# Four transposes instead of two in each small PSUM tile, and one wide copy out of it

## What is computed

```python
xn = _layernorm(x, axis=-1)
Q = xn @ W1 + b1;  K = xn @ W2 + b2;  V = xn @ W3 + b3
attn = softmax(Q @ K.T / sqrt(1024))          # 4096 x 4096 for each batch element
attn_out = (attn @ V) @ W4 + b4
# feed-forward on the same xn: two 512x512 matrices W_real, W_imag, unfolded from small factors
out_real = xn_real @ W_real.T - xn_imag @ W_imag.T + bias_real
out_imag = xn_real @ W_imag.T + xn_imag @ W_real.T + bias_imag
x = x + attn_out + concat(out_real, out_imag)
```

## Time and profile before

| | us |
|---|---|
| median of the runs | 1701.88 |
| the profiled execution, slowest core with what lies around its span | 1703.39 |
| its span, first to last instruction, slowest core (core 3) | 1701.8 |
| spans of the 8 cores | 1689.6 to 1701.8 |
| TensorE matmuls booked as busy | 1553.4 (91%) |
| VectorE | 757.2 (44%) |
| ScalarE | 483.5 (28%) |
| GpSimd | 128.7 (8%) |

### The profile page before, as it was taken

The page is one execution under the profiler, slowest core; times in us unless marked ns, Lnnn a source line. Parts: engine busy times, 40 slices in busy tenths (PEclk is TensorE's granted clock), DMA queues, the critical chain, the costliest instruction groups (busy, mean ns, idle before and its releaser), DMA issues.

```text
span 1701.8 us, 25375 instructions; the slowest of 8 cores (1689.6 to 1701.8 us)
## 1 busy us (share of the span) xinstructions
PE 1553.4 (91%) x8496; PEld 763.4 (45%) x8496; DVE 757.2 (44%) x1863; ACT 483.5 (28%) x873; POOL 128.7 (8%) x107
## 2 busy tenths in 40 slices
PE   1668899998999999999999999999999999999998
PEld 1323565655444444444444444444444444444443
DVE  3212332423455445535553555355445535553554
ACT  0101333333322222222332322322322232332322
POOL 2000111112000000000000000000000000000000
PEclk9859999999999999999999999999999999999999
DMA  9324121213311101111111110111101111110001
GB/s 177 48 62 40 73 75 51 75 50 100 87 38 44 45 26 61 39 38 38 38 38 38 38 50 26 50 38 38 50 26 54 47 38 38 38 38 26 26 26 38
DMA packets 69531, 83.48 MB, mean 49 GB/s; under 512 B 39699, under 2 KB 49947, under 8 KB 69406
## 3 DMA queue, kind: packets, MB, share of 16 engines
q1 hardware_dynamic: 56030, 42.01, 8.5%
q10 hardware_dynamic: 9216, 33.56, 6.0%
q0 software_dynamic: 4160, 6.29, 2.4%
HBM read 69.27 MB, written 18.87 MB: 52 GB/s over the span
## 4 chain that ended last, share of the span: by engine, by line
PE 89%; DVE 4%; DMA 2%; issue 2%; SPq 2%; ACT 1%; DVEq 0%; POOL 0%; ACTq 0%; POOLq 0%
PE po L659 13%; PE po L557 13%; PE po L663 13%; PE sp_a L557 7%; PE sp_b L557 6%; PE pf L588 3%; PE sp_a L422 3%; PE sp_a L524 3%; PE sp_b L422 3%; PE sp_b L524 3%; PE pf L446 3%; PE po L446 3%; PE ptA L630 2%; PE ptB L630 2%; DVE QXT L402 2%
## 5 line engine op out<-in xcount | busy, mean ns | idle before, releaser
L663 PE MATMUL po<-V,ETs 128*128 128x512 bf16 x1024 | 388.0, 379 | 0.0
L659 PE MATMUL po<-V,ETs 128*128 128x512 bf16 x1024 | 388.0, 379 | 0.0
L557 PE MATMUL po<-KT,QXT 128*128 128x512 bf16 x1024 | 231.5, 379 | 0.0
L618 DVE TENSOR_REDUCE r<-Et 128x1 f32<-128x512 bf16 x256 | 173.5, 678 | 31.6 <-ACT Et L614 31.4
L614 ACT ACTIVATE Et<-Ssb,ngm 128x512 bf16<-128x512 f32 x256 | 164.2, 709 | 57.6 <-DVE ngm L578 47.2
L378 POOL TENSOR_SCALAR xnn<-xg,rstd,nmr 128x1024 bf16<-128x1024 f32 x64 | 76.6, 1201 | 1253.6 <-DVE nmr L374 1253.6
L557 PEld LDWEIGHTS po<-KT,QXT 128*128 128x128 bf16 x1024 | 100.2, 98 | 120.8
L570 DVE TENSOR_REDUCE mx<-po 128x1 f32<-128x512 f32 x128 | 88.5, 692 | 132.7 <-ACT Ssb L567 132.7
L567 ACT ACTIVATE Ssb<-sp_a 128x512 f32<-128x512 f32 x64 | 38.2, 597 | 369.0 <-PE sp_a L557 369.0
L663 PEld LDWEIGHTS po<-V,ETs 128*128 128x128 bf16 x1024 | 100.0, 98 | 94.5
L659 PEld LDWEIGHTS po<-V,ETs 128*128 128x128 bf16 x1024 | 99.9, 98 | 94.5
(11 more groups left out here) (92 smaller groups left out, 1780.2 us busy)
## 6 DMA issues: line engine op xcount, KB each, us to landing
xg<-x ACTq DMA_DIRECT2D x64, 512.0 KB, 3.7
xr<-x SPq DMA_DIRECT2D x32, 512.0 KB, 3.5
out<-xr SPq DMA_DIRECT2D x32, 512.0 KB, 2.6
KT<-W POOLq DMA_DIRECT2D x2, 2048.0 KB, 49.6
Ssb<-W SPq DMA_DIRECT2D x8, 512.0 KB, 6.4
Wproj<-W POOLq DMA_DIRECT2D x1, 2048.0 KB, 25.7
scr<-V SPq DMA_DIRECT2D x2, 1024.0 KB, 4.5
V<-scr SPq DMA_DIRECT2D x64, 32.0 KB, 2.5
```

The source lines that it names most:

```text
L557: P.add("tensor", lambda e, tb=tb, c=c, si=si, spv=spv: e.matmul(spv, QT[:, c, si * 128:(si + 1) * 128], KT[:, c, tb * 512:(tb + 1) * 512] ...
L618: P.add("vector", lambda e, tb=tb: e.reduce_sum(r8[:, tb:tb + 1], Et[:, tb % 4, :], axis=AX.X), waits=[("exp", i, tb)] + ([("rr", i - 1)] ...
L659: P.add("tensor", lambda e, tb=tb, q=q, tj=tj: e.matmul(po[:, 0:512], ETs[:, tb % 4, q, :], V0[:, tj, 0:512], start=(tj == 0), stop=(tj == ...
L663: P.add("tensor", lambda e, tb=tb, q=q, tj=tj: e.matmul(po[:, 512:1024], ETs[:, tb % 4, q, :], V0[:, tj, 512:1024], start=(tj == 0), stop= ...
```

## The change

The small PSUM tiles grow from 128x256 to 128x512 bf16 (1024 bytes a partition, still within one bank each). `emit_ln_tps` fills ptA with four transposes and ptB with four, and copies each out with one 128x512 copy. `emit_tp` puts all four pieces of a block of E into one tile, ptA for even blocks and ptB for odd ones, and copies it with one 128x512 copy. Waits that named the fourth LN copy (number 3) name the second (number 1) in K, V, Q and F, and O waits for one `ete` mark instead of two. The transposes of W3 stay in pairs. The number of transposes and of all other instructions is unchanged.

```diff
-    ptA = E(nc.psum_tensor("ptA", [128, 2, 128], BF16))
-    ptB = E(nc.psum_tensor("ptB", [128, 2, 128], BF16))
+    ptA = E(nc.psum_tensor("ptA", [128, 4, 128], BF16))
+    ptB = E(nc.psum_tensor("ptB", [128, 4, 128], BF16))
...
-            waits=[("nmr", gt), ("xtp", gt - 2, 3) if gt >= 2 else None],
+            waits=[("nmr", gt), ("xtp", gt - 2, 1) if gt >= 2 else None],
...
-        for p4 in range(4):
-            bank, bk = (ptA, "ptA") if p4 % 2 == 0 else (ptB, "ptB")
-            c0 = 2 * p4
-            xw = [("lnap", gt), free[bk]] + (list(extra_tp) if p4 == 0 else [])
-            P.add("tensor", lambda e, c0=c0, slot=slot, bank=bank: e.transpose(
-                bank[:, 0, :], xnn[:, slot, c0 * 128:(c0 + 1) * 128], ident[:, :]),
-                waits=xw + [("id2",)], mark=None)
-            P.add("tensor", lambda e, c0=c0, slot=slot, bank=bank: e.transpose(
-                bank[:, 1, :], xnn[:, slot, (c0 + 1) * 128:(c0 + 2) * 128], ident[:, :]),
-                mark=("xtp", gt, p4))
+        for q2 in range(2):
+            bank, bk = (ptA, "ptA") if q2 == 0 else (ptB, "ptB")
+            c0 = 4 * q2
+            xw = [("lnap", gt), free[bk]] + (list(extra_tp) if q2 == 0 else [])
+            for qq in range(4):
+                P.add("tensor", lambda e, c0=c0, qq=qq, slot=slot, bank=bank:
+                      e.transpose(bank[:, qq, :],
+                                  xnn[:, slot, (c0 + qq) * 128:(c0 + qq + 1) * 128],
+                                  ident[:, :]),
+                      waits=(xw + [("id2",)]) if qq == 0 else [],
+                      mark=("xtp", gt, q2) if qq == 3 else None)
             P.add("vector", lambda e, u=u, c0=c0, bank=bank: e.tensor_copy(
-                xnT[:, u, c0:c0 + 2, :], bank[:, :, :]),
-                waits=[("xtp", gt, p4)], mark=("xte", gt, p4))
-            free[bk] = ("xte", gt, p4)
+                xnT[:, u, c0:c0 + 4, :], bank[:, :, :]),
+                waits=[("xtp", gt, q2)], mark=("xte", gt, q2))
+            free[bk] = ("xte", gt, q2)
         if phase == 2:
             P.add("gpsimd", lambda e, u=u: e.tensor_scalar_mul(
                 ngxT[:, u, :],
                 xnT[:, u, 4:8, :].rearrange("p c n -> p (c n)"), -1.0),
-                waits=[("xte", gt, 2), ("xte", gt, 3)], mark=("ngx", gt))
+                waits=[("xte", gt, 1)], mark=("ngx", gt))
...
-                      waits=[("xte", 4 * g + 2 * half + 1, 3), ("LW2",),
+                      waits=[("xte", 4 * g + 2 * half + 1, 1), ("LW2",),
                              free[spk]],
...
-                for h in range(2):
-                    bank, bk = (ptA, "ptA") if h == 0 else (ptB, "ptB")
-                    for qq in range(2):
-                        q = 2 * h + qq
-                        P.add("tensor", lambda e, tb=tb, q=q, qq=qq, bank=bank:
-                              e.transpose(bank[:, qq, :],
-                                          Et[:, tb % 4, q * 128:(q + 1) * 128],
-                                          ident[:, :]),
-                              waits=[("exp", i, tb), free[bk]] if qq == 0 else [],
-                              mark=("etp", i, tb, h) if qq == 1 else None)
-                    if tb >= 4:
-                        slotprev = ("Omm", i, tb - 4, 1)
-                    elif i >= 1:
-                        slotprev = ("Omm", i - 1,
-                                    NTB - 4 + tb if NTB >= 4 else 0, 1)
-                    else:
-                        slotprev = None
-                    P.add("vector", lambda e, tb=tb, h=h, bank=bank: e.tensor_copy(
-                        ETs[:, tb % 4, 2 * h:2 * h + 2, :], bank[:, :, :]),
-                        waits=[("etp", i, tb, h), slotprev],
-                        mark=("ete", i, tb, h))
-                    free[bk] = ("ete", i, tb, h)
+                bank, bk = (ptA, "ptA") if tb % 2 == 0 else (ptB, "ptB")
+                for q in range(4):
+                    P.add("tensor", lambda e, tb=tb, q=q, bank=bank:
+                          e.transpose(bank[:, q, :],
+                                      Et[:, tb % 4, q * 128:(q + 1) * 128],
+                                      ident[:, :]),
+                          waits=[("exp", i, tb), free[bk]] if q == 0 else [],
+                          mark=("etp", i, tb, 1) if q == 3 else None)
+                if tb >= 4:
+                    slotprev = ("Omm", i, tb - 4, 1)
+                elif i >= 1:
+                    slotprev = ("Omm", i - 1,
+                                NTB - 4 + tb if NTB >= 4 else 0, 1)
+                else:
+                    slotprev = None
+                P.add("vector", lambda e, tb=tb, bank=bank: e.tensor_copy(
+                    ETs[:, tb % 4, :, :], bank[:, :, :]),
+                    waits=[("etp", i, tb, 1), slotprev],
+                    mark=("ete", i, tb, 1))
+                free[bk] = ("ete", i, tb, 1)
 
             def emit_omm(tb):
-                ow = [("ete", i, tb, 0), ("ete", i, tb, 1), V0DONE]
+                ow = [("ete", i, tb, 1), V0DONE]
```

More of the change, by code:

```diff
@@ L269, in emit_pro_tail @@
             P.add("vector", lambda e, i=i, j0=j0, bank=bank: e.tensor_copy(
-                W3T[:, j0:j0 + 2, i * 128:(i + 1) * 128], bank[:, :, :]),
+                W3T[:, j0:j0 + 2, i * 128:(i + 1) * 128], bank[:, 0:2, :]),
                 waits=[("w3tp", p2)], mark=("w3te", p2))
@@ L449, in emit_v @@
                     start=(k == 0), stop=(k == 7)),
-                    waits=[("xte", 4 * g + u, 3), W3PDONE, free[pk]],
+                    waits=[("xte", 4 * g + u, 1), W3PDONE, free[pk]],
                     mark=("Vmm", g, u, h) if k == 7 else None)
@@ L526, in emit_q2 @@
                     xnT[:, :, k, :], start=(k == 0), stop=(k == 7)),
-                    waits=[("xte", gt3, 3), ("LW1", r), free[spk]],
+                    waits=[("xte", gt3, 1), ("LW1", r), free[spk]],
                     mark=("Qmm", g, r) if k == 7 else None)
@@ L583, in build_nc @@
             for o in range(2):
-                fw = [("xte", gt, 3), WQDONE, CBDONE, ("ones",), free["pf"],
+                fw = [("xte", gt, 1), WQDONE, CBDONE, ("ones",), free["pf"],
                       ("ngx", gt)]
```

## The result

The changed kernel takes 1659.07 us (median of 8 runs, 1656.76 to 1660.36) against 1702.12 us of the kernel before, a ratio of 0.9751 with a 95% interval of 0.974 to 0.9761. The forecast was 1662, the range 1656 to 1681. One of the ten executions of the changed kernel (1886.67 us, a die at 0.84 of the granted clock instead of 0.98) and two of the ten of the kernel before (1857.04 and 1972.89 us) are left out of the ratio; the median 1702.12 still has those two in it and is 1701.80 without them.

A forecast was written before the change was run, and what follows sets the result against it. TensorE's instruction stream and its standstills bound the kernel. Gains of 17.9+17.4+2.2+2.2 = 39.7 us off the profiled 1703.39 give 1663.7, with the median 1.5 lower: 1662 us, range 1656 to 1681.

The forecast's parts named there:

- the four stretches named: (a) to (d): LN transposes in attention, projection pairs, query tile starts, E transposes of tb 3; 39.7 us in all.
- The copy's price: A 512-wide bf16 VectorE copy out of PSUM takes 0.42 us, worked out from rows of other widths.
- The latencies: Last transpose's start to copy 0.33 us; second copy 0.08 before the first ends; copy's end to released transpose 0.15.
- (a): LN transposes in the attention stage, 28 times: O matmuls at 1.30 instead of 1.94 us, gain 0.64 each, 17.9 us.
- (b): Pairs of LN tiles in the projection stage, 14 counted: 1.64 instead of 2.88 us, gain 1.24 each, 17.4 us.
- The hidden pairs: Four of 18 projection pairs, two at the start, those at 165.76 and 415.40, gain nothing because other waits hide them.
- (c): Start of each query tile, 32 times: 1.07 instead of 1.14 us to the O matmuls, 2.2 us in all.
- (d): E transposes of tb 3, 28 times: 0.23 instead of 0.31 us, gain 0.08 each, 2.2 us.
- The cover at O of tb 2: The late copy releases O of tb 2 only 0.05 us before TensorE comes; beyond it each 0.1 us costs 2.8.
- The dearer copy: Rival: wide copy longer than 0.42 us, costing 88 us per us plus waits at tb 2; 1683 to 1700 us; chance 0.09.
- The swallowed projection gain: Rival: projection stage, faster TensorE meets x loads and normalisation, all of (b) is lost, 1680 us; chance 0.07.
- The clock: Rival: denser matmuls lower the granted clock; 2% over the run costs 33 us, 1695; chance 0.06 with another loss.

The follow-up runs named there:

- e2: Changed kernel with only the E half: LN transposes and copies in pairs as before the change; 1695.01 us, ratio 0.9955 to the kernel before.
- e3: Changed kernel with wide tiles kept, but each copied out in two 128x256 halves, as many copies as before the change; 1668.1 us, ratio 0.98.
- e4: Changed kernel plus one small unused VectorE copy behind the LN statistics at tb 1, in 28 tiles; 1666.51 us, ratio 0.9792.
- both further steps: Changed kernel with whole-bank ptA and ptB alternating between groups, and TP(0) moved inside the feed-forward matmuls; 1613.62 us in the second set, ratio 0.9477.
- e6: Changed kernel with a query tile's first E transposes, TP(0), moved inside the feed-forward matmuls; 1637.98 and 1639.74 us in two of four executions.
- e1: Changed kernel with only the LN half: E transposes and copies in pairs as before the change; 1671.01 us, ratio 0.9844.
- e8: Changed kernel run once more without an edit, beside the kernel with both further steps; 1659.66 us, ratio 0.9755.
- e5: Changed kernel with ptA and ptB of 128x1024 bf16, each transpose group taking the other tile than the one before; 1632.81 to 1634.33 us, ratio 0.9584.

## Why the prediction was right

**The bound.** TensorE's instruction stream and its stands: right. 40.6 of the 43.0 us are in the four stretches named. VectorE's 31 us less of booked time bought little by itself: e2 saves two thirds of the copies for 7.5 us, and e3 saves none and keeps 34 of the 43.

**The copy's price.** 0.42 forecast, 0.420 to 0.425 measured. The formula that the prediction quoted from the Trainium skill (VectorE: DVE Perf Modes, section on the TRN2 errata) gives 392 ns; the measurement decides for 420.

**The latencies.** 0.33 from the last transpose to the copy and 0.15 from the copy to TensorE carried over unchanged (the fourth transpose starts at 1013.81+0.17 = 1013.98, the copy at 1014.32; a copy ends at 1024.90+0.42 = 1025.32, the transposes it releases start at 1025.47). The second wide copy starts 0.34 behind the first in 27 of the 28 attention tiles; the tile shown is the odd one, with 0.46, and nothing waited for that copy there.

**(a)** 0.64 forecast, 0.675 measured, of which 0.02 are two odd tiles of before at 2.20. **(b)** 1.24 against 1.26 to 1.27 in a usual pair and 1.21 in three. The hidden pairs were named rightly: the one behind the first V projection kept 3.04 us in both kernels, and those at the start lie ahead of the bias wait, which grew from 15.7 to 18.8 us as they shrank. From the last pair, forecast at nothing, to the Q projection core 3 took 0.75 us less, but the mean of the eight cores did not fall (6.7 us before, 7.0 after). **(c)** and **(d)** came as forecast, with the wait of (c) now at O. The cover at O of tb 2 was 0.03 instead of 0.05 us, and e4 showed that it is as thin as said.

**The rivals.** The dearer copy fell with its length, but its slope was right: 88 us per us of copy and more at tb 2, of which e3 measured 9.0 for 0.07. The swallowed projection gain fell: ACT's ln step had 2.4 us to spare before, 1.10 after (statistics end at 311.48, the step starts at 312.58). In the kernel with both further steps it is used up at some pairs: ACT waits 0.30 us for the statistics at 304.74. The clock stayed at 1.00 in the attention stage; in the projection stage it did change, to the good.

**The size.** 39.7 us forecast, 43.0 between the spans, 42.7 between the medians (1701.80 and 1659.07). About 0.9 of the 3.3 us missing between the spans are in (a) to (d). The attention stage, up to its last matmul, gained 23.0 to 23.2 us on each of the eight cores (1255.5 to 1255.9 us before, 1232.4 to 1232.7 after), where (a), (c) and (d) had 22.3. The projection stage scatters: the attention stage starts at 427.8 to 439.8 us over the eight cores before (mean 434.3) and at 410.4 to 419.9 after (414.9). The means differ by 19.4 us with a standard error of about 1.8 (3.7 and 3.5 us of scatter over 8 cores each), against 17.4 forecast.

A term that the prediction left out explains most of these two microseconds: the granted clock in the projection stage. Behind the first V projections seven of the eight cores before have a stretch of 3.4 or 6.8 us at half the clock (core 3 from 178.2 to 185.0), after only core 3 (178.5 to 181.9). Count from the end of the pair at 165.76 to the start of the last pair. Before, core 5, which has no such stretch, took 243.6 us and the other seven 245.4 to 246.7; after, core 3 took 227.7 and the other seven 225.9 to 226.3. Between cores without such a stretch the fourteen pairs gained 17.5 us, against 17.4. In e2, which keeps the narrow LN tiles, all six cores at 0.98 of the clock have a stretch of 3.4 us; in the kernels with wide LN tiles none to four of eight have one (e6 none, e1 and e3 two, e8 three, e4 four). So these stretches are rarer with the wide LN tiles. Why they come at all stays open.

## What to carry to other kernels

When an engine writes small results that another carries off, price the whole loop: last write to copy, copy, copy to next write. Here it is 0.33+0.42+0.15 = 0.90 us against 0.23 us of transposes, so what matters is how many groups may be written before the first buffer is needed again; make each buffer larger, or alternate them across group kinds (e5 did both at once), and put other work into the loop. Wider copies help too, but by less. Measure a stall from start to start of the engine that sets the end: the idle time booked for the waits on small tiles fell from 57.3 to 36.8 us, only 20.5, where 40.6 were gained, since booked times overlap. And look for the place where a lightly booked engine has a dense run: 0.03 us of cover there is not seen in any average.

## What the runs showed that was not expected

A VectorE that is idle for more than half of the span passed 0.2 us of added work on with more than its own length: 28 copies of 195 ns, 5.5 us, cost 7.0 us in the stretch of TP(3), since each also brought the delay of its own wait ahead of it (statistics end at 1020.34, the copy starts at 1020.45 and the row sum behind it at 1020.56, 0.37 us behind the start of the last statistic; in the changed kernel it is 0.11).

With both further steps sixteen transposes into two tiles ran at 0.056 us each. The first copy out of `ptA` starts at 296.15, beside the last three of the transposes into `ptB` only, so this says little of a longer overlap of transposes and copy.
